# Second scan: GpSimd multiplies the feed of two of every eight units, in SBUF, in place of VectorE

## What is computed

```python
x_dbl = xs @ W_x                       # xs: the tokens, and the tokens reversed
delta = jax.nn.softplus(dts + b_dt)    # dts, Bs, Cs are cut from x_dbl
def step(hst, inp):
    d_t, u_t, B_t, C_t = inp
    dA = jnp.exp(d_t[:, :, None] * A)
    hst = dA * hst + (d_t * u_t)[:, :, None] * B_t[:, None, :]
    y_t = jnp.einsum('bdn,bn->bd', hst, C_t)
    return (hst, y_t)
y = y1 + y2[:, ::-1]
```

## Time and profile before

| | us |
|---|---|
| median of 3 runs | 1867.59 |
| lowest, highest | 1861.26, 1868.41 |
| the profiled execution | 1861.92 |
| its span | 1860.1 |
| second scan, first to last scan instruction of DVE | 465.5 to 1191.9 |
| PE, DVE, ACT, POOL busy over the span | 1513.1, 1544.7, 1198.4, 1081.5 |

### The profile page before, as it was taken

One profiled execution on the slowest core, in us unless ns is written; L12 is line 12 of the kernel. 1 busy time (PEld: TensorE's weight loads), 2 busy tenths in 40 slices (PEclk: granted clock), 3 DMA queues, 4 the chain that ended last, 5 costly groups with the idle time before them and its releaser, 6 DMA issues. The chain is left out here.

```text
span 1860.1 us, 29105 instructions
## 1 busy us (share of the span) xinstructions
PE 1513.1 (81%) x9958; PEld 776.7 (42%) x9958; DVE 1544.7 (83%) x1256; ACT 1198.4 (64%) x1852; POOL 1081.5 (58%) x702
## 2 busy tenths in 40 slices
PE   6999897998788788788778777568788888878688
PEld 3666545885333333333333333225333333333223
DVE  3778655545899999999999999663899999999955
ACT  5666584335677667766776666367767777776456
POOL 1777401000577777777777777400698999989601
PEclk8999997999899999999999998789899999999989
DMA  4000000000344544454445444400000000000001
GB/s 147 2 0 0 1 1 1 1 1 1 67 93 93 96 93 90 93 96 93 90 92 97 94 90 93 92 0 1 1 1 1 1 0 0 0 0 0 1 13 46
DMA packets 23296, 78.10 MB, mean 42 GB/s; under 512 B 3776, under 2 KB 4672, under 8 KB 22976
## 3 DMA queue, kind: packets, MB, share of 16 engines
q0 software_dynamic: 18288, 66.59, 18.9%
q1 hardware_dynamic: 4944, 10.68, 2.0%
HBM read 8.58 MB, written 2.10 MB: 6 GB/s over the span
## 5 line engine op out<-in xcount | busy, mean ns | idle before, releaser
L1184 POOL TENSOR_TENSOR s_prod<-s_ahead,s_cs 128x1024 f32<-128x1024 f32 x127 | 308.8, 2431 | 185.1 <-DVE s_back L1127 156.3
L2003 POOL TENSOR_TENSOR r_state<-r_state,r_cs 128x1024 f32<-128x1024 f32 x127 | 300.7, 2383 | 120.1 <-ACT r_cs L1889 100.9
L1954 DVE TENSOR_TENSOR_SCAN r_state<-r_decay,r_pu 128x1024 f32<-128x1024 f32 x128 | 292.7, 2287 | 13.7 <-PE r_py L1805 8.7
L1124 DVE TENSOR_TENSOR_SCAN s_ahead<-s_fore,s_pu 128x1024 f32<-128x1024 f32 x128 | 292.7, 2287 | 8.8 <-ACT s_fore L1041 1.8
L1127 DVE TENSOR_TENSOR_SCAN s_back<-s_aft,s_pu 128x1024 f32<-128x1024 f32 x128 | 289.5, 2261 | 1.2 <-ACT s_aft L1051 1.2
L1873 ACT ACTIVATE r_decay<-r_pd,r_aneg 128x1024 f32<-128x1024 f32 x128 | 142.7, 1115 | 101.0 <-PE r_pd L1747 100.6
L1041 ACT ACTIVATE s_fore<-s_pd,s_aneg 128x896 f32<-128x896 f32 x128 | 129.9, 1015 | 112.3 <-PE s_pd L854 111.1
L1747 PE MATMUL r_pu<-r_partsu,selr 64*128 64x512 f32 x512 | 156.3, 425 | 23.3 <-DVE r_state L1954 21.2
L854 PE MATMUL s_pu<-s_partsu,selr 64*128 64x512 f32 x512 | 98.1, 461 | 80.1 <-DVE s_back L1127 76.6
L1950 DVE TENSOR_TENSOR r_pu<-r_pu,r_bs 128x1024 f32<-128x1024 f32 x128 | 154.7, 1208 | 7.7 <-PE r_pu L1747 7.7
L1117 DVE TENSOR_TENSOR s_pu<-s_pu,s_bs 128x1024 f32<-128x1024 f32 x128 | 154.5, 1207 | 3.4 <-PE s_pu L854 3.4
(11 more groups left out here) (355 smaller groups left out, 3266.7 us busy)
## 6 DMA issues: line engine op xcount, KB each, us to landing
s_ahead<-s_back POOLq DMA_DIRECT2D x127, 512.0 KB, 4.5
x_act<-in_x_dram SPq DMA_DIRECT2D x8, 256.0 KB, 5.5
out_dram<-x_act SPq DMA_DIRECT2D x16, 128.0 KB, 2.3
k_fir<-in_pack_fir_dram SPq DMA_DIRECT2D x1, 1600.0 KB, 7.2
k_scan<-in_pack_scan_dram SPq DMA_DIRECT2D x1, 1600.0 KB, 10.6
k_l<-in_pack_l_dram SPq DMA_DIRECT2D x1, 515.0 KB, 4.4
k_l<-in_pack_l_dram SPq DMA_DIRECT2D x1, 450.0 KB, 11.2
k_ln<-in_pack_ln_dram SPq DMA_DIRECT2D x3, 131.0 KB, 3.1
```

Source lines behind the costliest of these rows:

```text
L1124: dve.tensor_tensor_scan(ahead[:, v % 4], f, feed[:], 0.0, ALU.mult, ALU.add).then_inc(ahead_done, 1)
L1184: pool.tensor_tensor(prod[:, b], ahead[:, v % 4], cs[:, buf].rearrange("p i n -> p (i n)"), ALU.mult).then_inc(prod_done, 1)
L1954: dve.tensor_tensor_scan(state[:, v % 4], decay[:, v % 4], feed[:], 0.0, ALU.mult, ALU.add).then_inc(scanned, 1)
L2003: pool.tensor_tensor(state[:, v % 4], state[:, v % 4], cs[:, phase, q // 2], ALU.mult).then_inc(multiplied, 1)
```

## The change

Units p with p % 8 equal to 0 or 2, from unit 2 on, take another way (`by_pool`), 31 of the 128:

- ACT copies `ps_u[0]` into `back[p % 4]` in SBUF, at step p+8, ahead of that unit's decays (`u_copied`).
- POOL, at step p+8, multiplies `back[p % 4]` by `bs` in place (`pool_fed`). In such a step it first executes a multiplication of one column (`tick`) and issues the sum of unit s-10, then the feed, and then the product of unit s-12.
- DVE leaves out its multiplication for these units, waits for `pool_fed`, and scans from `back[p % 4]` forwards into `ahead` and backwards in place. The backward scan now also waits for the forward one.
- `fed` is raised by 2 by the unit after, so its counts stay the same.

The lags, the buffers, and PE's program stay as they are.

```diff
+        u_copied, pool_fed = m.sem("s_ucop"), m.sem("s_poolfed")
+        tick = m.sb("s_tick", [P, 1])
+        def by_pool(p, v):
+            return v % 8 in (0, 2) and live(p, UNITS) and not (isinstance(p, int) and p < 2)
+        def pooled(p, v):
+            return p + v % 8
@@ ScalarE, before fore
+                if by_pool(p, v):
+                    act.wait_ge(u_rep, p + 1)
+                    wait(act, summed[0], 8 * p - 16)
+                    act.activation(back[:, v % 4], ps_u[0][:], ACT.Copy).then_inc(u_copied, 4)
@@ VectorE
+                    if by_pool(p, v):
+                        feed = back[:, v % 4]
+                        dve.wait_ge(pool_fed, pooled(p, v))
+                    else:
+                        dve.wait_ge(u_rep, p + 1)
+                        if v % 2 == 0 or v % 8 in (1, 3):
+                            dve.wait_ge(b_copied, p - v % 2 + 2)
+                        feed = ps_u[b]
+                        dve.tensor_tensor(feed[:], feed[:], bs[:, buf].rearrange("p i n -> p (i n)"),
+                                          ALU.mult).then_inc(fed, 2 if by_pool(p - 1, v - 1) else 1)
+                        dve.wait_ge(fed, p + 1)
                     dve.wait_ge(fore_done, p + 1)
                     wait(dve, prod_done, p - 3)
                     dve.tensor_tensor_scan(ahead[:, v % 4], f, feed[:], 0.0, ALU.mult, ALU.add).then_inc(ahead_done, 1)
                     dve.wait_ge(aft_done, p + 1)
+                    if by_pool(p, v):
+                        dve.wait_ge(ahead_done, p + 1)
@@ GpSimd
+                n, w = s - LAG_D, u - LAG_D
+                feeds = by_pool(n, w)
+                def add():
+                    pool.dma_start(ahead[:, z % 4], back[:, z % 4], accum_op=ALU.add).then_inc(summed[z % 2], 16)
+                if feeds:
+                    if live(f, UNITS - 1):
+                        wait(pool, summed[0], 8 * f)
+                        pool.tensor_tensor(tick[:], tick[:], tick[:], ALU.mult)
+                        add()
+                    pool.wait_ge(b_copied, n + 2)
+                    pool.wait_ge(u_copied, pooled(n, w))
+                    pool.tensor_tensor(back[:, w % 4], back[:, w % 4], bs[:, w % 4 // 2].rearrange("p i n -> p (i n)"),
+                                       ALU.mult).then_inc(pool_fed, 4)
                 if live(p, UNITS - 1):
                     ...
                     pool.tensor_tensor(prod[:, b], ahead[:, v % 4], cs[:, buf].rearrange("p i n -> p (i n)"),
                                        ALU.mult).then_inc(prod_done, 1)
-                if live(f, UNITS - 1):
-                    pool.dma_start(ahead[:, z % 4], back[:, z % 4], accum_op=ALU.add).then_inc(summed[z % 2], 16)
+                if live(f, UNITS - 1) and not feeds:
+                    add()
```

More of the change, by code:

```diff
@@ L1112, in body @@
                     b, buf = v % 2, v % 4 // 2
[L1113 to L1119, removed]
-                    f, a = fore[:, b].rearrange("p n t -> p (n t)"), aft[:, b].rearrange("p n t -> p (n t)")
-                    dve.wait_ge(fed, p + 1)
+                    f, a = fore[:, b].rearrange("p n t -> p (n t)"), aft[:, b].rearrange("p n t -> p (n t)")
+                    if by_pool(p, v):
[9 more added lines that the diff above has]
+                        dve.wait_ge(fed, p + 1)
                     dve.wait_ge(fore_done, p + 1)
@@ L1166, in _ @@
         def _(pool):
+            pool.memset(tick[:], 0.0)
             pool.memset(fore[:, :, :, 0:1], 0.0).then_inc(zeroed, 1)
```

## The result

| | us |
|---|---|
| before, median (lowest to highest of 4 runs) | 1868.0 (1861.3 to 1868.8) |
| changed, median (lowest to highest of 4 runs) | 1958.0 (1957.4 to 1964.6) |
| ratio, 95% interval | 1.0504 (1.0471 to 1.0537) |
| profiled execution of the changed kernel, its span | 1964.6, 1962.6 |

A forecast was written before the change was run, and what follows sets the result against it. DVE was taken to bound the second scan; 31 pooled units, each 2.65 us longer from stall and collision net of the removed feed multiply, sum to 82 us, giving 1949 us (range 1885 to 1978).

The forecast's parts named there:

- The bound and the leash: Second scan: DVE, 99% busy, is the bound; PE and POOL wait on its backward scans, so its losses are the kernel's.
- The stall: Before a pooled unit's forward scan, DVE waits 1.3 us for POOL's product of n-4, now behind the feed.
- the collision: Pooled scans, both operands in SBUF, and POOL's product of n-3 exclude each other: 2.39 us more per pooled unit.
- The wait between the scans: A pooled unit's backward scan must wait for its forward one: 0.12 to 0.18 us a unit, 4 to 6 in all.
- The whole pair: End of unit n-2's backward scan to end of pooled unit n's, D(n-2) to D(n): 13.9 us against 11.25 before.
- Late ACT in unit 2: Unit 2 of eight: ACT's softplus chain delays u's copy 0.8 us, plus 0.4; not felt with the collision.
- (b): Rival, chance 0.17: the collision does not come or costs little; +9 to 28 us, up to 45; 1877 to 1912.
- (c): Rival, chance 0.11: POOL's DMA issue (0.9 us) also delays the scan, or waits lengthen; 28 us more, 1961 to 1985.
- (d): Rival, chance 0.04: DVE's 1.25 us per pooled unit are really won, no collision; 34 us faster, 1834.
- The rule on shared access: Skill's rule: DVE with two SBUF inputs and POOL exclude each other; sum 82 us with it, 9 to 28 without.

The follow-up runs named there:

- e4_no_partner: Changed kernel with POOL's product of unit n-3, the one that meets the pooled forward scan, cut to one column; one run, 1892.6 us.
- e2_psum: Changed kernel, same order and waits, but DVE's scans of pooled units read u in PSUM, leaving out the product with B; 1898.4 us, ratio 1.0136.
- e3_order_psum: Changed kernel with POOL's product before the feed and pooled scans reading u in PSUM, without the product with B; 1866.0 us, ratio 0.9986.
- e1_order: Changed kernel with POOL's product put before the feed and the one-column multiplication left out; 1900.4 us, ratio to before 1.014.
- e5_decay_psum: Changed kernel with POOL's product before the feed, and ACT writing pooled units' forward decays into the PSUM bank u was copied from; 1913.4 us, ratio 1.0232.

## Why the prediction was right, point by point

- **The bound and the leash.** Right: outside the pooled units no D to D changed by more than 0.01 us, and every loss of DVE's came through to the end.
- **The stall.** Right in kind and undersized: 1.80 us where 1.33 was worked out. Measured over the 26 pooled units of the table above, link by link, against the sum: backward scan to PE 0.08 (0.10), PE's four matmuls **1.18 (0.74)**, to ACT 0.22 (0.04), copy **1.02 (1.11)**, to POOL 0.17 (0.15), feed, product and DVE's pick-up 4.76 (4.80); total 7.44 against 6.94. The mis-sized term is PE's. In 24 of the 26 units the four matmuls ran for 1.22 us at a granted clock of 0.50, the lower of the clock's two levels (1.2 GHz), as at 874.96, where PE had stood still for 2.14 us before; the prediction had given it 0.2 us in its range's end. In e4_no_partner, with the collision gone and shorter pauses, 4 of 26 took over 1 us (mean 0.78) and the granted clock of the window was 0.95 instead of 0.89. So the matmuls that DVE next waited for were slow more often where DVE stalled for longer. That the stall is what lowers the clock is not shown: ahead of unit 7 of eight PE stood still about as long in the changed kernel, 2.06 us, and all 13 ran at 0.73.
- **What the slow matmuls cost.** At most 31 x 0.44 = 14 us, and by the two units that ran at full clock less. In unit 0, number 88 had a gap of 1.26 us, the twelve others 1.75 to 1.94. In unit 2, number 82 had the longest gap of all, 2.23 us, because ACT took up u only 1.10 us after it was there:

```profile
991.68 0.73 PE L864 MATMUL s_pu<-s_partsu,selr 64*128 64x512 f32 x4
...
992.99 0.63 ACT L1087 ACTIVATE s_ex<-s_ex 128x512 f32<-128x512 f32 x1
...
993.51 1.02 ACT L1050 ACTIVATE s_back<-s_pu 128x1024 f32<-128x1024 f32 x1
```

  In e4_no_partner PE was fast in all 13 of these units and the gap was no shorter (1.88). So in unit 2 the late ACT stands right behind PE, and an estimate of the cost from unit 0 alone is 15 x 0.5 = 8 us.
- **The wait between the scans.** The sum had 0.05 us between them and 0.09 of overlap lost; measured are 0.20 and 0.09, and the waiting backward scan takes 2.29 us instead of 2.26: 0.18 a unit, 31 x 0.18 = 6 us too little.
- **The whole pair.** D(n-2) to D(n) is 14.3 us, where 13.9 was to be looked for: +0.47 in the stall, +0.18 between the scans, -0.25 in the collision. The errors cancel in part, and the medians lie 90 us apart where the pooled units of the two profiles make 95. That the result comes within 8 us of the 82 is partly luck.
- **The collision.** Right, and the one that decides: 2.14 us of the forward scan, 2.39 forecast, 31 x 2.14 = 66 us. It came short of a whole product since DVE was at the gate 0.1 to 0.2 us after POOL began, and ended 2.16 us after the product, less than the 2.29 of a whole scan. The 60 us between the changed kernel and e2_psum agree.
- **Late ACT in unit 2.** As forecast, not felt in the changed kernel (gaps 1.77 and 1.83), and felt as soon as the collision is gone (e2_psum 1.48 and 2.17, e4_no_partner 1.42 and 1.88; +0.5 to 0.7 where +0.8 to 1.2 stood). The reason given, that unit n-2 is itself late by more, is not all of it: in unit 82 ACT was late even so.
- **The rivals.** (b) would have been right with the scans in PSUM: e2_psum and e4_no_partner (one run) measured +30 and +24, just above and within its 9 to 28. (c) is out: the DMA issue stands behind the product (884.57 to 885.42 in the timeline above), and the scan goes on beside it and ends 2.16 us after the product. (d) would have needed both costs gone, and e3_order_psum shows that even then the 34 us aren't there.
- **The rule on shared access.** The Trainium skill ("SBUF — State Buffer", section "Who interferes with whom") says that a DVE instruction with two SBUF inputs contends with a GpSimd instruction that reads SBUF, that the one which issues first keeps the shared pair for its whole length, and that a DVE instruction with at most one SBUF input, outside its 2-port modes, doesn't contend. The runs agree in all three parts, for scans too: with two SBUF inputs scan and product exclude each other (e1_order), whichever comes second waits (4.21 and 4.13 us), and with one input in PSUM they don't meet (e5_decay_psum, a scan of 2.28 us beside the product).

## What to carry to other kernels

Before work is moved from VectorE to GpSimd, look where the operands will lie afterwards: an operand that moves from PSUM to SBUF can make two engines exclude each other, and the price is the other engine's instruction, not one's own. Look up on which finished step the receiving engine's other duties in the same step are awaited: work put in front of them is on their path. And take the bound away in an experiment before building the version (e3_order_psum): here the next chain, over PE, ACT and POOL, took 6.20 us in one unit of eight, where DVE's own work had taken 5.66, and the gain was gone.

## What the runs showed of the hardware that I had not expected

- A scan of 1024 elements takes 2.27 us, against 1.21 for a multiply, and holds POOL off for the whole of that time: POOL's product took 4.21 us. POOL, waiting, gets in between two scans of DVE that stand 0.20 us apart, as it did between two multiplies in the earlier trace rows.
- The profile puts the wait inside the instruction: it shows DVE busy for 4.4 us, and its idle time tells nothing of it. Only the duration by form (two kinds of one line) does.
- ACT copies 128x1024 from PSUM to SBUF in 1.02 us, less than the 1.11 of the exponential that I had taken for it.
